# A three-stage decoder: row sums by 32-column matmuls and a VectorE transpose, four expert weight sets loaded a stage earlier

## The chip, the core and the metric

The kernel runs on one core of one Trainium2 chip. The metric is device time in microseconds of one launch; lower is better. Before the change three runs gave a median of 1043.18 us (1040.03 to 1043.35).

## What is computed

A post-layer-norm decoder layer for x of 4 batches, 512 tokens, 512 features, float32, in three sublayers, each followed by a residual add and a layer norm:

```python
x = _layernorm(x + _L0_attn_ref(x, Wq, bq, Wk, bk, Wv, bv))       # 16 heads of 32: window of 256 keys, all keys for 64 chosen queries
x = _layernorm(x + _L0_xattn_ref(ctx_512, ctx_512, mask, pad_mask, x, Wq, bq, Wk, bk))   # softmax(scores * x), 512x512 per batch
x = _layernorm(x + _L0_ffn_ref(x, gate_w, w_gate, w_up, w_down, sw_gate, sw_up, sw_down))  # top 2 of 8 experts of width 352, and a shared one of 704
```

Softmax needs the sum of each row of exponentials. In attention there are 512 rows and 16 heads per batch, and the sums divide the product of probabilities and values.

## The kernel before

The program has four blocks, one after the other, each with its own list of instructions for every engine, ordered by semaphores: `project` (projections of queries, keys, values and context), `attend`, `cross_and_shared` and `experts`.

**attend** (from L615) works through 16 units, each a batch and a group of 4 heads. Keys lie on partitions. In a unit, TensorE (`unit`, L820) has 16 steps. Step s computes one 128x512 block of transposed scores (L830, called st here), which ScalarE turns into exponentials `probs` (L892); beside it stands one 128x512 block of plain scores (L772) of a unit ahead, of which VectorE takes the maxima (L920, `reduce`), five blocks of them (`EARLY`) one unit further ahead. The maxima of all 16 blocks become shift rows (`row_maxima`, L923), which TensorE turns (`turn`, L775) and ScalarE copies into the queries (`take_shift`). The score blocks go round three PSUM banks. `RING` is 17: the seventeenth place of a unit is used for its row sums (`rows_bank`), so each unit's first two scores wait for the score two before them and its third for the reciprocal.

At chosen steps TensorE also does the finishing work of the unit before. `weigh` (L783) is the value product, 4 matmuls with 32 stationary columns each, that go to four column groups of the array. `sums` (L794) adds up the exponentials: GpSimd adds pairs of probability blocks (L719), and 4 matmuls with a stationary block of ones give every row sum 32 times over, laid out as the output is. The trace shows a float32 matmul as two records. ScalarE copies output and sums to SBUF (`take_out` L874, `take_sum` L879). `back` (L805) then brings both back to tokens on partitions: four transposes of the output (L813), and four matmuls with a 0/1 matrix that pick one sum per head (L812). VectorE takes reciprocals and multiplies (`normalise`, L946).

The order, by step: step 3, `weigh(u-1, 3)` and `sums(u-1, 0)`; step 7, `sums(u-1, 1)`; step 11, `back(u-1)` and `weigh(u, 0)`; step 15, `turn(u+1)`, `weigh(u, 1)`, `weigh(u, 2)`.

**cross_and_shared** goes through 16 tiles of 128 tokens. SP's queue per tile: store of x2 (L1204), load of the input of the tile after next (L1196), store of x3 (L1212). GpSimd reads the input in `add_attn` (L1229), then computes masks and the roots of the layer norms in order. After the last tile SP loads the weights of expert 0 (`load_expert`, L1086: four DMAs, together 2.1 MB).

**experts** goes through 39 tiles of 128 gathered rows, sorted by expert. SP first issues ten lists of rows (L1755), waits for the first four gathers, and loads experts 1 to 7, each when the one before has landed (L1763 to L1766). GpSimd issues the gathers (L1791) and the scatter-adds (L1797) and clears the unused rows of the weights (L1808). ScalarE and VectorE split the weights of each tile into two halves (L1825, L1893), ScalarE applies the gate activation (L1833), TensorE does 33 matmuls and 7 transposes a tile.

The attention results, the context parts (`qk_ctx`) and, in the first two blocks, the values `v` share SBUF with `w_all`, the weights of all experts.

## Time and profile before

| what | value |
|---|---|
| median of 3 runs | 1043.18 us (1040.03 to 1043.35) |
| the profiled execution's own time | 1040.61 us |
| its span in the trace | 1038.9 us |
| TensorE busy (PE) | 929.5 us, 89% |
| VectorE busy (DVE) | 750.2 us, 72% |
| ScalarE busy (ACT) | 594.4 us, 57% |
| GpSimd busy (POOL) | 523.3 us, 50% |
| attention stage | about 180 to 449 us |
| cross and shared stage | about 449 to 713 us |
| expert stage | about 713 to 1039 us |
| mean granted TensorE clock | 0.954 |

A share of the whole span says little here, as the stages have different limits; a stage is read from its own stretch. Start and length of an instruction are in microseconds from the start of the span. In the timeline equal neighbours are merged: "x8" is eight records from the first's start to the last's end. Matmuls are pipelined, so the distance of two starts, not a length, is the cost of one.

### The profile page before, as it was taken

How to read it: one execution, taken by the hardware profiler on the slowest of the kernel's cores; microseconds unless marked ns; L12 is line 12 of the kernel's file. 1: busy time of each engine (PE TensorE's matmuls, PEld its weight loads, DVE VectorE, ACT ScalarE, POOL GpSimd, SP SyncE). 2: the span in 40 equal slices, each digit the busy share in tenths (PEclk: the TensorE clock that was granted, in tenths of full speed). 3: DMA queues.
4: the chain of work that ended last, by engine and by line, in shares of the span. 5: the costliest groups of instructions: out<-in, count | busy, mean ns of one | idle time of the engine just before them, and what ended most of it. 6: DMA issues, size and time to landing. Idle time of an engine off the chain costs nothing. (4 is left out here: it accounts for less than half of the span.)

```text
span 1038.9 us, 18144 instructions
## 1 busy us (share of the span) xinstructions
PE 929.5 (89%) x5112; PEld 715.9 (69%) x5112; DVE 750.2 (72%) x1348; ACT 594.4 (57%) x914; POOL 523.3 (50%) x532
## 2 busy tenths in 40 slices
PE   7999997899999999938999999992887999999980
PEld 5777885455554545417988888982876998988970
DVE  4427555777777777459888888744877999999983
ACT  4533211677767777725434434431866888888863
POOL 3550001466666666455555665524143667786634
PEclk9999998899999999968999999996999999999995
DMA  8657301625344256011111111132798444444476
GB/s 280 241 190 224 142 1 38 143 64 121 92 90 120 62 121 186 28 33 64 63 62 62 41 51 61 51 115 49 235 274 231 74 70 79 81 71 73 79 184 212
DMA packets 80885, 115.73 MB, mean 111 GB/s; under 512 B 15681, under 2 KB 37057, under 8 KB 80833
## 3 DMA queue, kind: packets, MB, share of 16 engines
q1 hardware_dynamic: 68960, 93.58, 30.4%
q0 software_dynamic: 9760, 20.49, 10.9%
q10 hardware_dynamic: 2112, 1.05, 0.4%
q8 instruction: 23, 0.38, 0.2%
q14 instruction: 30, 0.24, 0.1%
HBM read 74.77 MB, written 40.31 MB: 111 GB/s over the span
## 5 line engine op out<-in xcount | busy, mean ns | idle before, releaser
L1893 DVE TENSOR_TENSOR we_lo<-w_all,we_hi 128x1408 fp32r<-128x1408 f32 (+1 forms) x117 | 192.6, 1674 | 13.6 <-ACT we_hi L1825 12.9
L920 DVE TENSOR_REDUCE maxima<-ps_s 128x8 f32<-128x512 f32 x240 | 148.9, 684 | 54.7 <-PE ps_s L772 54.5
L1825 ACT ACTIVATE we_hi<-w_all 128x1408 fp32r (+1 forms) x117 | 165.9, 1421 | 37.0 <-PE e_ps_y L1966 20.1
L719 POOL TENSOR_TENSOR pair_sum<-probs 128x512 f32<-128x512 f32 x120 | 150.0, 1279 | 68.9 <-ACT probs L892 68.9
L892 ACT ACTIVATE probs<-ps_st 128x512 f32<-128x512 f32 x256 | 134.3, 602 | 56.5 <-PE ps_st L830 54.9
L1797 POOL DMA_INDIRECT x_dram<-e_y,who x39 | 103.2, 2646 | 124.8 <-ACT e_y L1842 80.0
L1563 PE MATMUL ps_gu<-sw_hi,x2T_hi 128*128 128x352 f32 (+1 forms) x256 | 87.7, 343 | 2.6 <-issue 1.7
L1563 PE MATMUL ps_gu<-sw_lo,x2T_hi 128*128 128x352 f32 (+1 forms) x256 | 83.7, 327 | 0.0
L1563 PE MATMUL ps_gu<-sw_hi,x2T_lo 128*128 128x352 f32 (+1 forms) x256 | 83.4, 326 | 0.0
L772 PE MATMUL ps_s<-k_more,q_more 96*128 96x512 f32 x160 | 67.9, 429 | 4.1 <-DVE maxima L920 2.2
L1791 POOL DMA_INDIRECT xg<-x_dram,who x39 | 61.2, 1568 | 14.3 <-issue 11.1
L830 PE MATMUL ps_st<-q_more,k_more 128*128 128x512 f32 x160 | 67.5, 424 | 0.2 <-ACT probs L892 0.2
L790 PE MATMUL ps_o<-probs,vu 128*32 128x512 f32 x512 | 64.8, 601 | 0.0
L830 PEld LDWEIGHTS ps_st<-q_more,k_more 128*128 128x128 f32 x160 | 30.1, 189 | 40.8 <-issue 23.9
L1966 PE MATMUL e_ps_g<-we_hi,xgT_hi 128*128 128x352 f32 x156 | 55.0, 353 | 3.3 <-DVE we_lo L1893 3.3
L343 DVE SCALAR_TENSOR_TENSOR qk_ctx<-ps_proj,bias_qk,qk_ctx 128x512 fp32r<-128x512 f32 x32 | 24.0, 751 | 46.0 <-ACT attn L276 28.4
L1966 PE MATMUL e_ps_u<-we_hi,xgT_hi 128*128 128x352 f32 x156 | 53.8, 345 | 0.0
L270 ACT ACTIVATE qk_ctx<-ps_proj,bias_qk 128x512 fp32r<-128x512 f32 x32 | 22.1, 689 | 54.8 <-PE ps_proj L457 53.9
L1563 PEld LDWEIGHTS ps_gu<-sw_hi,x2T_hi 128*128 128x128 f32 x256 | 48.7, 190 | 5.5 <-issue 3.5
L1966 PE MATMUL e_ps_g<-we_lo,xgT_hi 128*128 128x352 f32 x156 | 51.9, 332 | 0.0
L1966 PE MATMUL e_ps_g<-we_hi,xgT_lo 128*128 128x352 f32 x156 | 51.7, 332 | 0.0
L1340 ACT ACTIVATE act_g<-ps_gu 128x352 f32<-128x352 f32 x32 | 14.9, 464 | 62.9 <-PE ps_gu L1563 62.6
(272 smaller groups left out, 2484.3 us busy)
## 6 DMA issues: line engine op xcount, KB each, us to landing
qk_dram<-qk_ctx SPq DMA_DIRECT2D x32, 512.0 KB, 3.0
q_more<-qk_dram SPq DMA_DIRECT2D x60, 128.0 KB, 3.0
k_more<-qk_dram SPq DMA_DIRECT2D x60, 128.0 KB, 3.1
w_all<-in_L_ffn_w_gate_dram SPq DMA_DIRECT2D x8, 704.0 KB
w_all<-in_L_ffn_w_up_dram SPq DMA_DIRECT2D x8, 704.0 KB
q_first<-qk_dram SPq DMA_DIRECT2D x36, 128.0 KB, 3.2
k_first<-qk_dram SPq DMA_DIRECT2D x36, 128.0 KB, 3.4
x_tile<-in_x_dram SPq DMA_DIRECT2D x16, 256.0 KB, 2.7
```

What stands on the lines that cost most here:

```text
L719: last = pool.tensor_tensor(pair_sum[:, h, j], probs[:, 2 * h, j], probs[:, 2 * h + 1, j], ALU.add)
L772: pe.matmul(bank(p, x), q4[p][0:BR, j, t * P:(t + 1) * P], k4[p][0:BR, j, :], start=True, stop=True).then_inc(s_done, 1)
L790: last = pe.matmul(ps_o[HD * j:HD * (j + 1), :], vu[:, kc, HD * j:HD * (j + 1)], probs[:, kc, j, :], start=(kc == 0), stop=(kc == TT - 1))
L830: pe.matmul(st_bank(p, s), k4[p][:, j, kc * P:(kc + 1) * P], q4[p][:, j, :], start=True, stop=True).then_inc(st_done, 1)
L892: act.activation(probs[:, kc, j, :], st_bank(p, s), ACT.Exp, scale=SCALE).then_inc(exp_done, 1)
L920: dve.tensor_reduce(by_tile[:, t, j, 1:9], bank(p, x).rearrange("p (g n) -> p g n", n=S // 8), axis=AX.X, op=ALU.max).then_inc(s_reduced, 1)
L1563: last = pe.matmul(out, stationary[a](q), moving[z](q), start=(q == 0 and k == 0), stop=(q == chunks - 1 and k == 2))
L1791: pool.indirect_dma_start(out=xg[:, j % XG, :], out_offset=None, in_=x2_dram[:], in_offset=bass.IndirectOffsetOnAxis(ap=who[:, j, 0:1], ax ...
L1797: pool.indirect_dma_start(out=x3_dram[:], out_offset=bass.IndirectOffsetOnAxis(ap=who[:, j, 0:1], axis=0), in_=y[:, p, :], in_offset=None, ...
L1825: act.activation(w_hi[kind][:], raw(base, kind), ACT.Copy).then_inc(s[kinds[kind] + "_hi"], 1)
L1893: dve.tensor_tensor(w_lo[kind][:], raw(base, kind), w_hi[kind][:].bitcast(F32), ALU.subtract).then_inc(s[kinds[kind] + "_lo"], 1)
L1966: last = pe.matmul(out, stationary[a](q), moving[z](q), start=(q == 0 and k == 0), stop=(q == chunks - 1 and k == 2))
```

## The change

In attention the row sums are computed once per row instead of 32 times: the stationary operand is one column of ones among 32 (`head_col`), one for each head, and each of 4 column groups takes 128 tokens, so the sums of all four heads and all tokens lie in a 128x128 block. VectorE transposes its 32x32 blocks to `sum_rows` and takes the reciprocal; ScalarE's copy and the four matmuls of `back` go. The bank place for the row sums goes too, so scores use all three banks without exception. The second `sums` moves from step 7 to step 11, ahead of `weigh(u, 0)`, and `back` from step 11 to step 15, ahead of `turn`. VectorE's row work is split in two, with the first reduction of the next unit in between, and the normalisation moves behind that unit's first five reductions.

SBUF is laid out anew: `v` first (over the space of the early loads), then the context parts batch by batch, then the attention results; `w_all` begins behind the gather buffers `xg`. Experts 0, 1, 2 and 3 are loaded in the cross stage, ahead of SP's work for tiles 2, 12, 14 and 15; experts 4 to 7 in the expert stage as before. The unused rows are cleared in two halves, the kept experts' at the end of the cross stage, the others' behind the fourth gather.

```diff
+def ctx_at(which, part, b):
+
+    return b * (4 * S) + (2 * which + part) * S
...
-        ones = m.sb("ones_sum", [P, HD])
+        head_col = m.sb("head_col", [P, HPG, HD])
         probs = m.sb("probs", [P, TT, HPG, S])
         pair_sum = m.sb("pair_sum", [P, 2, HPG, S])
         outT = m.sb("outT", [P, S])
-        sumT = m.sb("sumT", [P, S])
-        first_rows = m.sb("first_rows", [P, HPG])
+        sum_rows = m.sb("sum_rows", [P, TT, HD])
...
+        ps_total = ps_sum[:, 0:P]
...
-            return ps_s[:, (RING * p + x) % BANKS, :]
-
-        def rows_bank(p):
-
-            return bank(p, NU)[:, 0:TT * HPG].rearrange("p (t j) -> p t j", j=HPG)
+            return ps_s[:, (NU * p + x) % BANKS, :]
...
-                pool.memset(ones[:], 1.0)
                 pool.memset(turn_in[:], 0.0)
-                pool.memset(first_rows[:], 0.0).then_inc(cleared, 1)
+                pool.memset(head_col[:], 0.0).then_inc(cleared, 1)
                 pool.wait_ge(cleared, 1)
-                pool.affine_select(out=first_rows[:], in_=first_rows[:], compare_op=ALU.not_equal, fill=1.0, base=0,
-                                   pattern=[[-HD, HPG]], channel_multiplier=1).then_inc(cleared, 1)
+                for j in range(HPG):
+                    last = pool.memset(head_col[:, j, j:j + 1], 1.0)
+                last.then_inc(cleared, 1)
...
-                    if x < 2:
-                        need(pe, s_reduced, NU * u + x - 1)
-                    elif x == 2:
-                        need(pe, recip_done, u - 2)
-                    else:
-                        need(pe, s_reduced, NU * u + x - BANKS + 1)
+                    need(pe, s_reduced, NU * u + x - BANKS + 1)
                     pe.matmul(bank(p, x), q4[p][0:BR, j, t * P:(t + 1) * P], k4[p][0:BR, j, :],
...
-                        last = pe.matmul(ps_sum[HD * j:HD * (j + 1), :], ones[:], pair_sum[:, h, j, :],
-                                         start=(h == 0), stop=(h == 1))
+                        rows = pair_sum[:, h, j, :].rearrange("p (t a i) -> p a t i", t=TT, i=HD)
+                        for a in range(P // HD):
+                            last = pe.matmul(ps_total[HD * a:HD * (a + 1), :], head_col[:, j, :], rows[:, a],
+                                             start=(h == 0 and j == 0), stop=(h == 1 and j == HPG - 1))
                     last.then_inc(sums_done, 1)
-                def back(u, after, scores):
+                def back(u):
                     pe.wait_ge(o_taken, u + 1)
                     pe.wait_ge(sum_taken, u + 1)
-                    pe.wait_ge(normed, u + 1)
-                    pe.wait_ge(s_reduced, scores)
                     for t in range(TT):
-                        pe.matmul(rows_bank(after)[:, t, :], sumT[:, t * P:(t + 1) * P], first_rows[:], start=True, stop=True)
                         last = pe.transpose(ps_back[:, t * P:(t + 1) * P], outT[:, t * P:(t + 1) * P], c.ident[:])
                     last.then_inc(backed, 1)
...
                         if s == 3 and not first:
                             weigh(u - 1, 3)
                             sums(u - 1, 0)
-                        if s == 7 and not first:
-                            sums(u - 1, 1)
                         if s == 11:
                             if not first:
-                                back(u - 1, (p + 1) % SLOTS, NU * U if last else NU * (u + 1) + 14)
+                                sums(u - 1, 1)
                             weigh(u, 0)
                         if s == 15:
+                            if not first:
+                                back(u - 1)
                             if not last:
                                 turn(u + 1, p)
                             weigh(u, 1)
...
                         sums(u, 0)
                         weigh(u, 3)
                         sums(u, 1)
-                        back(u, (p + 2) % SLOTS, NU * U)
...
+                        back(u)
...
-                def take_sum(u):
-                    act.wait_ge(sums_done, 2 * u + 2)
-                    act.activation(sumT[:], ps_sum[:], ACT.Copy).then_inc(sum_taken, 1)
...
                 def row_maxima(u):
-                    k = [0]
+                    dve.wait_ge(s_reduced, NU * u + NU)
+                    dve.tensor_reduce(m_win[:].rearrange("p t j -> p t j"), windows, axis=AX.X, op=ALU.max)
+                    dve.tensor_reduce(m_all[:], by_tile, axis=AX.X, op=ALU.max).then_inc(row_step, 1)
+
+                def turn_rows(u):
+
+                    k = [1]
                     def step(ins):
                         k[0] += 1
...
                         dve.wait_ge(row_step, 6 * u + k[0])
                     bar = c.bar[:, :, bass.ds(HPG * u, HPG)]
-                    dve.wait_ge(s_reduced, NU * u + NU)
-                    dve.tensor_reduce(m_win[:].rearrange("p t j -> p t j"), windows, axis=AX.X, op=ALU.max)
-                    step(dve.tensor_reduce(m_all[:], by_tile, axis=AX.X, op=ALU.max))
+                    dve.wait_ge(row_step, 6 * u + 1)
                     step(dve.tensor_tensor(m_bar[:], m_all[:], bar, ALU.add))
                     step(dve.tensor_tensor(m_row[:], m_bar[:], m_win[:], ALU.max))
                     need(dve, turned, u)
...
                     step(dve.tensor_copy(bar_rows, bar))
                     dve.sem_inc(turn_ready, 1)
-                def normalise(u, after):
+                def take_sum(u):
+                    dve.wait_ge(sums_done, 2 * u + 2)
+                    dve.transpose(sum_rows[:].rearrange("p t r -> p (t r)"), ps_total).then_inc(sums_turned, 1)
+                    dve.wait_ge(sums_turned, u + 1)
+                    dve.sem_inc(sum_taken, 1)
+                    dve.reciprocal(rsum[:], sum_rows[:, :, 0:HPG]).then_inc(recip_done, 1)
+
+                def normalise(u):
                     dve.wait_ge(backed, u + 2)
-                    dve.reciprocal(rsum[:], rows_bank(after)).then_inc(recip_done, 1)
                     dve.wait_ge(recip_done, u + 1)
                     dve.tensor_tensor(slot(c.attn, u).rearrange("p (t w) -> p t w", w=HD), ps_back[:].rearrange("p (t w) -> p t w", w=HD),
                                       rsum[:].rearrange("p t (j a) -> p (t j) a", a=1).to_broadcast([P, TT * HPG, HD]),
...
                         for x in range(EARLY, NU):
                             reduce(u + 1, (p + 1) % SLOTS, x)
                         row_maxima(u + 1)
+                        if not (isinstance(u, int) and u > U - 3):
+                            dve.wait_ge(row_step, 6 * (u + 1) + 1)
+                            reduce(u + 2, (p + 2) % SLOTS, 0)
+                        turn_rows(u + 1)
+                        if not first:
+                            take_sum(u - 1)
                     else:
                         last_pairs(0)
-                    if not first:
-                        normalise(u - 1, (p + 1) % SLOTS)
+                        take_sum(u - 1)
                     if last:
+                        normalise(u - 1)
                         last_pairs(1)
                     if not (isinstance(u, int) and u > U - 3):
-                        for x in range(EARLY):
+                        for x in range(1, EARLY):
                             reduce(u + 2, (p + 2) % SLOTS, x)
+                    if not first and not last:
+                        normalise(u - 1)
                     if last:
-                        normalise(u, (p + 2) % SLOTS)
+                        take_sum(u)
+                        normalise(u)
                 dve.sem_inc(s_reduced, NU)
                 dve.wait_ge(cleared, 1)
                 row_maxima(0)
+                turn_rows(0)
...
+def unused_rows(c, first, end):
+
+    return c.w_all[FCR:P, first * WCOLS:end * WCOLS].rearrange("p (e n) -> p e n", n=WCOLS)[:, :, WCOLS - D:WCOLS]
...
+                def expert_in(e):
+                    if e:
+                        sp.wait_ge(c.w_in, 64 * e)
+                    load_expert(sp, c, e, w_gate, w_up, w_down, c.w_in)
+
                 def one(n, b, t):
+                    if isinstance(n, int) and n == 2:
+                        sp.wait_ge(s["sw_split"], 6)
+                        expert_in(0)
+                    if isinstance(n, int) and n == NT - TT:
+                        sp.wait_ge(s["sc_done"], 2 * TT)
+                        sp.wait_ge(s["q_tile_done"], 2 * TT)
+                        expert_in(1)
+                    if isinstance(n, int) and n == NT - 2:
+                        sp.wait_ge(s["sc_done"], NT)
+                        sp.wait_ge(s["q_tile_done"], NT)
+                        expert_in(2)
+                    if isinstance(n, int) and n == NT - 1:
+                        sp.wait_ge(s["x3_st"], 16 * n - 16)
+                        expert_in(3)
...
                 tiles(sp, one)
-                sp.wait_ge(s["sc_done"], NT)
-                sp.wait_ge(s["q_tile_done"], NT)
-                load_expert(sp, c, 0, w_gate, w_up, w_down, c.w_in)
...
                 tiles(pool, one)
+                pool.wait_ge(s["sw_split"], 6)
+                pool.wait_ge(s["sc_done"], NT)
+                pool.wait_ge(s["x3_st"], 16 * (NT - 2))
                 pool.iota(plan_tiles.at_i, pattern=[[P, NT]], base=0, channel_multiplier=0)
                 pool.iota(plan_tiles.tile_i, pattern=[[1, NJ]], base=0, channel_multiplier=0).then_inc(s["plan_built"], 1)
                 send(NT - 1, (NT - 1) % 2)
+                pool.memset(unused_rows(c, 0, KEPT), 0.0)
...
+KEPT = 4
...
-                for e in range(1, E):
-                    list_in(e + LISTS - 1, (e + LISTS - 1) % WHO)
+                for e in range(KEPT, E):
+                    list_in(e + LISTS - KEPT, (e + LISTS - KEPT) % WHO)
                     sp.wait_ge(c.w_in, 64 * e)
                     load_expert(sp, c, e, w_gate, w_up, w_down, c.w_in)
-                first = E + LISTS - 1
+                first = E + LISTS - KEPT
...
-                    if j == 1:
+                    if j == 3:
                         pool.wait_ge(s["padded"], 1)
                         pool.wait_ge(half_done, 1)
-                        pool.memset(w[FCR:P, :].rearrange("p (e n) -> p e n", n=WCOLS)[:, :, WCOLS - D:WCOLS], 0.0).then_inc(s["zeroed"], 1)
+                        pool.memset(unused_rows(c, KEPT, E), 0.0).then_inc(s["zeroed"], 1)
...
+                    if isinstance(j, int) and j == 2:
+                        act.wait_ge(s["zeroed"], 1)
...
-                act.wait_ge(s["zeroed"], 1)
...
-            c.w_all = Memory(nc, later).sb("w_all", [P, E * WCOLS])
+            ml = Memory(nc, later)
+            c.xg = ml.sb("xg", [P, XG, D])
+            c.w_all = ml.sb("w_all", [P, E * WCOLS])
         with ExitStack() as ctx2:
             m2 = Memory(nc, ctx2)
-            c.qk_ctx = [[m2.sb(f"qk_ctx{a}{b}", [P, B * S], F32R) for b in range(2)] for a in range(2)]
-            c.attn = m2.sb("attn", [P, U, S])
             with ExitStack() as early:
                 me = Memory(nc, early)
                 c.x2 = me.sb("x2", [P, 2, D])
                 c.x_tile = me.sb("x_tile", [P, 2, D])
                 c.sw_raw = me.sb("sw_raw", [P, RAW, FC * D])
+            c.v = m2.sb("v", [P, U, TT * P])
+            c.ctx_parts = m2.sb("ctx_parts", [P, B * 4 * S], F32R)
+            c.attn = m2.sb("attn", [P, U, S])
             with ExitStack() as ctx3:
                 m3 = Memory(nc, ctx3)
-                c.v = m3.sb("v", [P, U, TT * P])
```

Left out: the same renaming of `qk_ctx` to `ctx_parts` at its other uses, and of arguments that fell away.

## Rows read from the trace of the kernel before

**Rows 1.** Busy time by stage; columns: stretch, each engine with its instructions, clock, DMA share.

```profile
180.00:449.00 269.00, 257.15 (x1520) 130.40 (x1520) 190.22 (x393) 189.90 (x352) 159.15 (x135) 0.98 0.42 101
...
713.00:803.00 90.00, 69.40 (x379) 63.15 (x380) 63.32 (x60) 58.76 (x68) 32.76 (x22) 0.89 0.77 224
```

**Rows 2.** Timeline of TensorE (PE, weight loads PEld) in one unit: start, length, count.

```profile
232.63 0.40 PE L780 MATMUL ps_st<-ident_bf,turn_in 128*128 128x128 bf16 x4
232.95 1.92 PE L790 MATMUL ps_o<-probs,vu 128*32 128x512 f32 x16
...
238.76 0.50 PE L830 MATMUL ps_st<-q_first,k_first 128*128 128x512 f32 x1
...
240.51 0.40 PE L772 MATMUL ps_s<-k_more,q_more 96*128 96x512 f32 x1
240.84 1.07 PE L801 MATMUL ps_sum<-pair_sum,ones_sum 128*32 128x512 f32 x8
240.84 0.16 PEld L801 LDWEIGHTS ps_sum<-pair_sum,ones_sum 128*32 128x32 f32 x8 [0.38 <-issue]
241.84 0.50 PE L830 MATMUL ps_st<-q_first,k_first 128*128 128x512 f32 x1
242.17 0.39 PE L772 MATMUL ps_s<-k_more,q_more 96*128 96x512 f32 x1
...
243.95 0.50 PE L772 MATMUL ps_s<-k_more,q_more 96*128 96x512 f32 x1 [0.20 <-DVE maxima L920]
244.29 0.28 PE L812 MATMUL ps_s<-first_rows,sumT 128*128 128x4 f32 x2
...
246.52 0.50 PE L830 MATMUL ps_st<-q_first,k_first 128*128 128x512 f32 x1
...
248.89 0.40 PE L780 MATMUL ps_st<-ident_bf,turn_in 128*128 128x128 bf16 x4
```

**Rows 3.** Timeline of VectorE (DVE) in the same unit.

```profile
242.60 1.89 DVE L920 TENSOR_REDUCE maxima<-ps_s 128x8 f32<-128x512 f32 x3 [0.59 <-PE ps_s L772]
...
245.11 0.17 DVE L936 TENSOR_TENSOR m_bar<-m_all,bar_kept 128x16 f32<-128x16 f32 x1
...
246.21 0.26 DVE L948 RECIPROCAL rsum<-ps_s 128x16 f32<-128x16 f32 x1
...
247.21 2.48 DVE L920 TENSOR_REDUCE maxima<-ps_s 128x8 f32<-128x512 f32 x4
```

**Rows 4.** Timeline of TensorE in the expert stage, transposes.

```profile
805.86 0.60 PE L1959 MATMUL e_ps_xT<-ident,xg 128*128 128x128 f32 x4
...
808.35 0.49 PE L1986 MATMUL e_ps_gT<-ident,e_g 128*128 128x128 f32 x3
```

**Rows 5.** Timeline of ScalarE (ACT) behind the last unit.

```profile
445.16 0.60 ACT L881 ACTIVATE sumT<-ps_sum 128x512 f32<-128x512 f32 x1 [0.26 <-PE ps_sum L801]
```

**Rows 6.** Timeline of SP's DMA issues, first and last late expert of seven.

```profile
729.30 0.43 SPq L1090 DMA_DIRECT2D w_all<-in_L_ffn_w_gate_dram  x1
...
788.28 0.37 SPq L1090 DMA_DIRECT2D w_all<-in_L_ffn_w_gate_dram  x1
```

**Rows 7.** Timeline of ScalarE in the expert stage, gate activations.

```profile
749.16 0.47 ACT L1833 ACTIVATE e_act<-e_ps_g 128x352 f32<-128x352 f32 x1 [0.34 <-PE e_ps_g L1966]
...
775.21 0.47 ACT L1833 ACTIVATE e_act<-e_ps_g 128x352 f32<-128x352 f32 x1 [0.43 <-DMA w_all<-in_L_ffn_w_down_dram]
...
808.61 0.47 ACT L1833 ACTIVATE e_act<-e_ps_g 128x352 f32<-128x352 f32 x1 [0.42 <-PE e_ps_g L1966]
...
815.45 0.46 ACT L1833 ACTIVATE e_act<-e_ps_g 128x352 f32<-128x352 f32 x1 [0.40 <-PE e_ps_g L1966]
```

**Rows 8.** Timeline of GpSimd (POOL) at the start of the expert stage.

```profile
719.45 3.51 POOL L1808 MEMSET w_all<- 32x4096 f32 x1
```

**Rows 9.** Timeline of SP's DMA issues in the cross stage, input of tile 4.

```profile
497.09 0.43 SPq L1196 DMA_DIRECT2D x_tile<-in_x_dram  x1
```

**Rows 10.** Timeline of GpSimd, where that input is read.

```profile
503.89 1.28 POOL L1229 TENSOR_TENSOR r<-x_tile,attn 128x512 f32<-128x512 f32 x1
```

22 lines of the change are left out of this document (10 added, 12 removed).

## The prediction

> **What bounds the kernel now.** I read the busy shares by stage first, then one attention unit instruction by instruction on TensorE and on VectorE, then the expert stage tile by tile, and last the queues that feed it. TensorE is busy 257 of the 269 us of attention, but only 69 of the first 90 us of the expert stage, where the DMA engines are at 0.77 [rows 1]. So the one stage is a matter of TensorE's order, the other of transfers.
>
> A unit of attention runs from one group of turned shifts to the next, 232.63 to 248.89, 16.26 us [rows 2]; twelve such units stand in a row. TensorE has hardly a gap in it. Three pieces are touched. The second sums, alone between two score steps, take 240.84 to 241.84. Eight narrow records last 1.07 and sixteen 1.92, so eight stream for 0.86; the other 0.14 is the change in and out. The score at 243.95 is late: VectorE's maxima release it. The back group, row-sum matmuls and transposes in turn, starts at 244.29, and with a value product behind it (0.86 and 0.14) it reaches the next step at 246.52: 1.23 us of its own. VectorE does three reductions in 1.89 us and four in 2.48, so 0.60 apart and 0.69 alone, and between 244.49 and 247.21 has a serial tail of maxima, rows, reciprocal and normalisation [rows 3].
>
> **The attention part.** I follow the unit from its step 4, 238.76.
> - Steps 4 to 11 now run without sums between them. A step costs TensorE 0.47 ((240.51 - 238.76 - 0.33)/3, the first score coming 0.33 after its step) and VectorE 0.60, so the reductions bind. The first score is at 239.09, its reduction 0.43 later as at 242.17 and 242.60 [rows 2, 3]. With the bank slot for the row sums gone every score needs the reduction three before it, the eighth the fifth: 239.52 + 4 x 0.60 + 0.69 = 242.61, so it starts at 242.67. Before it was at 243.95, less 1.00 of sums 242.95. Gain 0.28.
> - The second sums now stand directly ahead of the first value product: 242.67 + 0.33 (as 240.51 to 240.84) = 243.00, then 2 x 0.86 + 0.12: step 12 at 244.84, not 246.52 [rows 2]. In this are the 1.23 of the back group and 0.14 for the change that falls away.
> - VectorE decides what is left. Its last reduction ends at 239.52 + 6 x 0.60 + 0.69 = 243.81. The maxima take 0.62 with their wait (244.49 to 245.11 before). The first reduction of the next unit now slips in, 244.43 to 245.12; the rest of the rows 1.10 (245.11 to 246.21), to 246.15; then the new transpose of the sums and the reciprocal, 0.26 [rows 3]. The transpose is in no row. It moves 128 elements a partition: at least the 0.26 of the reciprocal's 16, at most the 0.69 of a whole bank's reduction. I take 0.31, since its size is nearer the small end, and 0.1 for its own wait. The second reduction ends at 246.15 + 0.41 + 0.26 + 0.69 = 247.51. Step 15's score needs it: 247.55, not 244.84 + 0.33 + 3 x 0.47 = 246.6. So 0.9 us of the gain become a wait for VectorE.
> - Four transposes go ahead of the turn. Four take 0.60 and three 0.49 in the expert stage [rows 4], so each costs 0.11: 0.45 in place of 1.23. Turn at 247.55 + 0.34 + 0.45 = 248.34, not 248.89: **0.55 us a unit**, 8.3 for fifteen.
> - ScalarE loses a copy of 0.60 a unit that nobody waits for inside the loop. At the very end it is on the path: 0.60 and the wait of 0.26 ahead of it [rows 5] and 0.78 of the back group, less 0.5 for the transpose and its wait: 1.1.
> - The sums stream as many columns, but in 16 logical matmuls of 128 a call instead of 4 of 512: 32 records, not 8. If the four column groups still stream side by side that is 0.86 again. I add 0.05 a call; the second call's surplus lies under the wait just named (cover 0.9), the first one's doesn't: 16 x 0.05 = 0.8. The other end: the back group's twelve small records take 1.23, 0.10 each, so 3.3 a call.
> Attention: 8.3 + 1.1 - 0.8 = **8.6 us less**. In the last unit the normalisation of unit 14 waits for transposes four steps later and stands ahead of the last pair sums on VectorE; two value products and the first sums on TensorE cover it. I cost it at nothing; uncovered it is about 0.7 once.
>
> **The weights.** Before, expert 0 is loaded behind the cross stage and experts 1 to 7 from 729.30 on, the last issued at 788.28: 9.8 us apart [rows 6]. An undisturbed tile takes 6.84 (gate activations 808.61 to 815.45 [rows 7]). From 749.16 to 775.21 three tiles take 26.05, 5.5 too many; from 775.21 to 808.61 four take 33.40, 6.0 too many: gathers and scatter-adds queue behind weights. Now experts 1 to 3 come in the cross stage and four remain. POOL's memset of 3.51 us [rows 8] moves behind the first four gathers at half its size, and SP, which waits for these gathers ahead of its loads, starts some 3 us earlier; four loads end near 766. The first loss stays, the second goes: **6.0 us less**. Bounds: 11.5 if both go, 0 if the loss only moves.
> The earlier loads share SP's queue with the cross stage. Ahead of tile 2, four issues of 0.6 and some 9 us of data (an expert's spacing, [rows 6]) now precede an input load that was issued at 497.09 and read at 503.89 [rows 9, 10]. From about 495.5 that makes it land near 507, 3 us late. POOL's chain for the next tiles, VectorE's normalisation and TensorE's transposes follow it. The same comes again ahead of tile 12; tiles 14 and 15 load no input. Price: 0 to 6 us. I take **2 us more**, as each stage of the chain has some room and TensorE is its last. The memset for the kept experts (half of 3.51) lies beside VectorE's table planning.
>
> **Sum.** -8.6 - 6.0 + 2 = -12.6. The profiled execution took 1040.61 us (span 1038.9), so 1028.0. It lies 2.6 below the median of the runs, 1043.18, and 0.6 above the fastest; the next median lies up to 2.6 above its sum. I forecast 1029.
>
> **The rivals.**
> - Short matmuls don't overlap (slower). Place: the 32 records of each sums call. For the cheap price: a call's eight weight loads last 0.16 together [rows 2], so eight are issued at once; no row shows 32. At 0.10 each a call takes 3.3, 2.4 more: 16 first calls pay 39, 16 second ones 1.5 each behind the cover, 24; 1029 + 63 = 1092. It decides from about 1.75 us a call, 55 ns a record: 16 x 0.9 = 14 eat the gain. Chance 0.09 beyond that, 0.03 close to it.
> The Trainium skill, "TensorE: Matmul & The Clock Gate" (Back-to-back issue gap), speaks for this rival: with hardware decode off the sequencer spends about 62 ns on each MATMUL, which binds for short ones. By it a call takes 32 x 0.062 = 1.98 us and the whole 1029 + 18 + 4 = 1051. The eight loads at once are against it, but a queue filled in advance would look the same.
> - VectorE's chain is longer: a transpose of 0.69, or a larger wait for it. Each 0.4 costs 15 x 0.4 = 6: 1035. Chance 0.08.
> - The prefetch only moves the collisions: the experts gain nothing and the cross stage loses 5: 1029 + 6 + 3 = 1038. For it: rows 7 show that a tile suffers wherever weights flow. Against: the intervals are 6.84 as soon as the loads end. Chance 0.10.
> - The loads come no earlier, as SP waits for the shared weights' split or an old store: 1029 + 6 - 2 = 1033. Chance 0.02.
> The forecast itself, 1022 to 1034, has 0.68.
>
> **Numbers.** A measurement of this kernel tells 0.3%, about 3 us, from no change. Faster: 0.68 + 0.08 + 0.10 + 0.02 = 0.88, less 0.04 for causes unseen: 0.84. Same 0.06, slower 0.10. The range goes from 1019 (both expert losses gone and no price in the cross stage) to 1040 (chain or collisions, and the runs' spread); some 0.12 lie above, 0.06 below.
>
> **What would show it.** Right: a unit of 15.6 to 15.8 us; a sums call of 0.9; at step 15 a score released by VectorE's maxima; gate activations 6.84 apart from about 767 of the old clock on; expert loads behind the stores of tiles 1, 11 and 13 in the cross stage; input reads of tiles 4 and 14 released by a DMA. Wrong: sums records more than 0.05 apart; a unit over 16; tiles that lose 1.5 us behind the last late load; two or more long tiles in the cross stage.

## The result and the profile after

Four runs of the changed kernel gave a median of 1031.66 us (1030.36 to 1032.52); four runs of the kernel before beside them, 1042.00. The ratio is 0.9901, 95% interval 0.9879 to 0.9924: about 10 us faster. The forecast was 1029.0, in a range of 1019 to 1040. The profiled execution took 1031.16 us, its span 1029.5. The busy times of each engine over the span follow; the shares say as little as before, only ScalarE has visibly less to do (594.4 us before):

```profile
PE 917.3 (89%) x5752; PEld 726.0 (71%) x5752; DVE 751.7 (73%) x1364; ACT 583.5 (57%) x898; POOL 533.0 (52%) x535
```

A unit of attention in the middle of the loop, as TensorE's timeline of the changed kernel shows it (start, length, engine, line, operation, tile, count, idle before and its releaser), to be held against [rows 2]:

```profile
235.29 0.39 PE L778 MATMUL ps_st<-ident_bf,turn_in 128*128 128x128 bf16 x4
...
240.43 1.06 PE L801 MATMUL ps_sum<-pair_sum,head_col 128*32 128x128 f32 x32
...
248.89 0.40 PE L770 MATMUL ps_s<-k_more,q_more 96*128 96x512 f32 x1
250.19 0.51 PE L770 MATMUL ps_s<-k_more,q_more 96*128 96x512 f32 x1 [0.67 <-DVE maxima L910]
250.53 0.60 PE L810 MATMUL ps_sum<-ident,outT 128*128 128x128 f32 x4
250.97 0.39 PE L778 MATMUL ps_st<-ident_bf,turn_in 128*128 128x128 bf16 x4
```

Turn to turn it takes 15.68 us, where it was 16.26. The 32 small records of a sums call last 1.06, as the eight large ones did (1.07). The score of step 15 is released by VectorE's maxima, and the four transposes take 0.44 to the turn. VectorE in the same stretch, against [rows 3]:

```profile
247.68 0.17 DVE L930 TENSOR_TENSOR m_bar<-m_all,bar_kept 128x16 f32<-128x16 f32 x1
...
248.44 0.20 DVE L937 CAST turn_in<-bar_kept 128x16 bf16 x1
248.87 0.32 DVE L942 STREAM_TRANSPOSE sum_rows<-ps_sum 128x128 f32<-128x128 f32 x1 [0.24 <-DVE turn_in L937]
249.33 0.25 DVE L945 RECIPROCAL rsum<-sum_rows 128x16 f32<-128x16 f32 x1
249.50 2.43 DVE L910 TENSOR_REDUCE maxima<-ps_s 128x8 f32<-128x512 f32 x4
```

The chain is the predicted one: rows, transpose, reciprocal, then the reduction that the score waits for.

The start of attention is not as predicted. The first unit, in the timelines of VectorE, GpSimd and TensorE of the changed kernel:

```profile
199.47 1.16 DVE L934 SCALAR_TENSOR_TENSOR turn_in<-m_row,turn_in 128x16 bf16<-128x16 f32 x1
...
199.25 3.78 POOL L722 TENSOR_TENSOR pair_sum<-probs 128x512 f32<-128x512 f32 x3 [3.65 <-ACT probs L885]
...
201.59 0.50 PE L770 MATMUL ps_s<-k_more,q_more 96*128 96x512 f32 x1 [1.64 <-DVE maxima L910]
202.26 2.90 PE L788 MATMUL ps_o<-probs,vu 128*32 128x512 f32 x16
```

The next turn stands at 201.93. A row step that takes 0.23 elsewhere takes 1.16 beside a pair addition of GpSimd; TensorE stands idle for 1.64; then sixteen records of the value product take 2.90 instead of 1.92. The first unit takes 22.0 us (19.95 before), the second 17.3 (16.25 before). Busy time by stretch shows the clock; the columns are those of [rows 1], and the stretches are the second unit, the unit shown above, and the middle stage:

```profile
201.93:219.24 17.31, 16.61 (x138) 9.45 (x138) 12.02 (x27) 11.26 (x21) 10.11 (x9) 0.90 0.37 83
235.29:250.97 15.68, 15.01 (x138) 8.84 (x136) 12.18 (x27) 11.14 (x21) 10.24 (x10) 1.00 0.35 99
...
461.94:680.63 218.69, 211.59 (x1190) 189.32 (x1191) 175.61 (x456) 94.69 (x170) 125.39 (x200) 0.98 0.27 85
```

In the middle stage the loads of expert 0 and expert 1 delay the input, as GpSimd's timeline says of tile 4 and of tile 14 (against [rows 10]). Between the two stands a second wait, on VectorE in tile 2, for GpSimd's small writes to the table of rows (`table_dram`) to land. The start of each tile on ScalarE, the x2 copies of tiles 2 and 3 and of tiles 12 and 13, shows what they cost:

```profile
499.56 1.29 POOL L1259 TENSOR_TENSOR r<-x_tile,attn 128x512 f32<-128x512 f32 x1 [1.67 <-DMA x_tile<-in_x_dram]
505.05 0.17 DVE L1514 TENSOR_REDUCE slot_u<-placed 128x2 uint32<-128x16 f32 x1 [2.72 <-DMA table_dram<-entry,slot_u]
...
645.62 1.29 POOL L1259 TENSOR_TENSOR r<-x_tile,attn 128x512 f32<-128x512 f32 x1 [4.04 <-DMA x_tile<-in_x_dram]
...
492.37 0.59 ACT L1369 ACTIVATE x2T_hi<-ps_xT 128x512 fp32r<-128x512 f32 x1
507.73 0.59 ACT L1369 ACTIVATE x2T_hi<-ps_xT 128x512 fp32r<-128x512 f32 x1
...
636.43 0.59 ACT L1369 ACTIVATE x2T_hi<-ps_xT 128x512 fp32r<-128x512 f32 x1
653.22 0.59 ACT L1369 ACTIVATE x2T_hi<-ps_xT 128x512 fp32r<-128x512 f32 x1
```

Tile 2 takes 15.36 us (14.27 before), tile 12 takes 16.79 (13.44 before). Tile 3 gives 0.4 back and tile 13 gives 0.7, so the two pairs of tiles cost 0.7 and 2.6. In tile 2 the wait that ends last is the one for the table's writes: the normalisation behind it starts at 505.44, and GpSimd's roots for it were ready at 504.65. The clock is not part of it: in both places it stays at 1.00. From first to last of these copies the stage takes 218.7, before 215.3. In the expert stage the gate activations keep the first loss of [rows 7] and are free of the second:

```profile
745.12 0.47 ACT L1868 ACTIVATE e_act<-e_ps_g 128x352 f32<-128x352 f32 x1 [0.34 <-PE e_ps_g L2002]
756.63 0.47 ACT L1868 ACTIVATE e_act<-e_ps_g 128x352 f32<-128x352 f32 x1 [2.67 <-PE e_ps_g L2002]
765.27 0.47 ACT L1868 ACTIVATE e_act<-e_ps_g 128x352 f32<-128x352 f32 x1 [1.39 <-PE e_ps_g L2002]
772.70 0.47 ACT L1868 ACTIVATE e_act<-e_ps_g 128x352 f32<-128x352 f32 x1 [1.01 <-PE e_ps_g L2002]
```

The 9.4 us between the two spans, by such marks: up to the last turn 3.9 gained, from there to the first x2 copy 2.2 gained, middle stage 3.3 lost, from there to the first gate activation 0.5 lost, gate activations 5.1 gained, the end behind the last of them 2.2 gained (35.2 us after 37.4).

### The profile page after: what moved, and what is told of

It reads as the page before. It is cut to its first block and busy times, and to the rows that moved or that the text cites. A ratio compares the mean times of both kernels' runs of the same rounds, so it can differ in the third digit from the quotient of the medians.

```text
span 1029.5 us, 19458 instructions
## 1 busy us (share of the span) xinstructions
PE 917.3 (89%) x5752; PEld 726.0 (71%) x5752; DVE 751.7 (73%) x1364; ACT 583.5 (57%) x898; POOL 533.0 (52%) x535
## 3 DMA queue, kind: packets, MB, share of 16 engines
q10 hardware_dynamic: 2112, 1.05, 0.4%
## 5 line engine op out<-in xcount | busy, mean ns | idle before, releaser
L1929 DVE TENSOR_TENSOR we_lo<-w_all,we_hi 128x1408 fp32r<-128x1408 f32 (+1 forms) x117 | 192.4, 1673 | 12.6 <-ACT we_hi L1860 11.7
L1832 POOL DMA_INDIRECT x_dram<-e_y,who x39 | 105.8, 2714 | 110.2 <-ACT e_y L1877 80.1
L885 ACT ACTIVATE probs<-ps_st 128x512 f32<-128x512 f32 x256 | 132.2, 604 | 51.4 <-PE ps_st L827 51.0
L1826 POOL DMA_INDIRECT xg<-x_dram,who x39 | 67.6, 1733 | 14.8 <-issue 11.1
L350 DVE SCALAR_TENSOR_TENSOR ctx_parts<-ps_proj,bias_qk,ctx_parts 128x512 fp32r<-128x512 f32 x32 | 24.0, 750 | 46.0 <-ACT attn L283 28.3
L277 ACT ACTIVATE ctx_parts<-ps_proj,bias_qk 128x512 fp32r<-128x512 f32 x32 | 22.1, 690 | 54.7 <-PE ps_proj L464 53.9
L770 PEld LDWEIGHTS ps_s<-k_more,q_more 96*128 96x128 f32 x160 | 31.5, 198 | 30.4 <-DVE maxima L910 23.5
```

Of the source, the lines that this page charges most:

```text
L770: pe.matmul(bank(p, x), q4[p][0:BR, j, t * P:(t + 1) * P], k4[p][0:BR, j, :], start=True, stop=True).then_inc(s_done, 1)
L885: act.activation(probs[:, kc, j, :], st_bank(p, s), ACT.Exp, scale=SCALE).then_inc(exp_done, 1)
L1826: pool.indirect_dma_start(out=xg[:, j % XG, :], out_offset=None, in_=x2_dram[:], in_offset=bass.IndirectOffsetOnAxis(ap=who[:, j, 0:1], ax ...
L1832: pool.indirect_dma_start(out=x3_dram[:], out_offset=bass.IndirectOffsetOnAxis(ap=who[:, j, 0:1], axis=0), in_=y[:, p, :], in_offset=None, ...
L1929: dve.tensor_tensor(w_lo[kind][:], raw(base, kind), w_hi[kind][:].bitcast(F32), ALU.subtract).then_inc(s[kinds[kind] + "_lo"], 1)
```

## The experiments

Below, "unit" is the time from turn to turn inside the loop, "middle stage" the time from the first to the last x2 copy, both from the one profiled execution of each kernel, and the time is the median of all runs with the ratio to the kernel before beside it. The kernel before gave medians of 1041.8 to 1042.6 in these comparisons, single runs 1036 to 1049.

### Each part alone

The first kernel is the one before with the edits to `attend` alone, the second the one before with all the other edits.

> The kernel before with the attention's part of the change alone: the new form and places of the row sums, the transposes at step 15, the new VectorE order, the scores' waits; the buffers' layout and all of the experts' loads stay as before. Theory (the two parts add up, and the attention's share is what the changed kernel shows up to its first x2 norm, which came 6.0 us earlier): about 1036.0, between 1035 and 1037.5, experts' part unchanged from before (gate activations lose 4.7 us at the fifth and 1.7 to 2.7 at three later ones). The two slow first units (22.0 and 17.3 us from turn to turn, where before had 19.95 and 16.25) should be here too if they come from the new order of the steps. Rival (the slow first units come from the moved buffers and the TensorE clock's luck): they are as before here, and the time is 3 us lower, about 1033.

Measured: 1035.03 us (1031.45 to 1036.98), ratio 0.9925 (0.990 to 0.995), inside the theory's range. Units 15.7; first x2 copy at 459.2, before at 468.0, 8.7 earlier. The first unit is slow here too (21.0), the second is not (15.7). The middle stage is as before (215.6).

> The kernel before with the other part alone: buffers laid out anew, the weights of experts 0 to 3 loaded among the tiles of the middle stage, the attention as before. Theory (the parts add up; middle stage +4, experts -5, and the final tail of 2.2 us belongs to the experts' loads): about 1038, between 1036.5 and 1039.5. Rival (the loads only take the places of other traffic, and the final 2.2 us come from elsewhere): 1040 to 1042, no change. Units of attention should take 16.26 us each from turn to turn, as before.

Measured: 1043.87 us (1038.92 to 1047.50), ratio 1.0006 (0.9985 to 1.0027). The rival fits, though the time lies even above its range: alone, the earlier loads bring nothing. In the profiled execution the gate activations take 269.6 us instead of 273.7, 4.1 gained, but the middle stage takes 222.5, 7.2 lost: tiles 2 and 3 take 17.75 and 14.86, tiles 12 and 13 take 17.03 and 13.71. So the attention's edits carry some 8 of the 10 us, and the loads between nothing and 3: the intervals of the ratios allow no closer split.

### What limits a unit now

```diff
                         turn_rows(u + 1)
+                        if not (isinstance(u, int) and u > U - 3):
+                            reduce(u + 2, (p + 2) % SLOTS, 1)
                         if not first:
                             take_sum(u - 1)
...
-                        for x in range(1, EARLY):
+                        for x in range(2, EARLY):
```

> The changed kernel with one more step of VectorE's order moved: the second score reduction of the unit after next goes ahead of the transposing copy and the reciprocal of the row sums, so the score of step 15 no longer waits for them. Theory (the 0.83 us that TensorE waits there each unit lie on the path, and VectorE has the room): the score starts 0.6 to 0.7 us earlier, a unit of 15.7 us becomes 15.0 to 15.2, time 1021 to 1025. Rival (VectorE's chain as a whole bounds a unit, so the wait moves to the next score or to the transposes behind the row sums' copy, now later): units stay at 15.6 to 15.7, time 1030 to 1033.

Measured: 1026.64 us (1022.44 to 1029.61), ratio 0.9841 (0.9814 to 0.9868). Units of 15.17: the wait was on the path and VectorE has the room. From first to last turn it is 10.0 us less than in the changed kernel. The time lies between the two expectations and is not 10 lower, because the middle stage took 224.3 here, with tiles 2 and 3 at 18.6 and 15.0: GpSimd waits 5.5 us for the input there, 1.7 in the changed kernel. Busy time by stretch around that stall shows the clock:

```profile
495.50:499.40 3.90, 0.54 (x5) 0.54 (x6) 1.27 (x3) 0.00 (x0) 2.81 (x5) 1.00 0.00 0
499.40:502.80 3.40, 3.40 (x11) 2.63 (x10) 2.19 (x6) 0.84 (x3) 1.47 (x4) 0.50 0.53 159
```

TensorE worked for 0.54 of 3.9 us and then went on at half clock (1.2 GHz) for 3.4 us. Tiles 2 and 3 take 4.5 us more than in the changed kernel. The wait for the input is 3.8 longer, and 3.4 us at half clock give away 1.7 by an estimate, so the wait is the larger part and the clock the smaller one. Why the input lands so much later here, the runs leave open.

The sums calls doubled:

```diff
-                            last = pe.matmul(ps_total[HD * a:HD * (a + 1), :], head_col[:, j, :], rows[:, a],
-                                             start=(h == 0 and j == 0), stop=(h == 1 and j == HPG - 1))
+                            for twice in range(2):
+                                last = pe.matmul(ps_total[HD * a:HD * (a + 1), :], head_col[:, j, :], rows[:, a],
+                                                 start=(h == 0 and j == 0 and twice == 0),
+                                                 stop=(h == 1 and j == HPG - 1 and twice == 1))
```

> The changed kernel with each of the 32 small matmuls of a row-sum call issued twice into the same accumulation, so the row sums come out doubled; all else as it is. It prices the call. Theory (a call of 32 records takes 0.87 to 0.90 us of TensorE's own time at steps 3 and 11, and both places are on the path that sets a unit): twice 0.8 to 0.9 more a unit, periods of 17.3 to 17.5 us, time 1055 to 1058. Rival 1 (only one of the two places is on the path, the other has cover in VectorE's reductions): periods of 16.5, time 1043 to 1046. Rival 2 (records queue up behind their own weight loads and are dearer when there are more): over 1060.

Measured: 1055.22 us (1051.79 to 1058.17), ratio 1.0117 (1.0087 to 1.0147). TensorE's timeline of one unit:

```profile
239.41 2.00 PE L802 MATMUL ps_sum<-pair_sum,head_col 128*32 128x128 f32 x64
245.66 2.02 PE L802 MATMUL ps_sum<-pair_sum,head_col 128*32 128x128 f32 x64
```

64 records last 2.00 and 32 last 1.06, so 0.94 for 32, 29 ns each. The unit is 16.63, 0.94 longer than 15.69, for two such additions: one call is on the path and the other is covered, as the first rival has it. It is the second that is covered: from turn to second call this unit takes 11.39 (10.46 in the changed kernel), and from there to the next turn 5.23 (5.22). The time of 1055 lies in the theory's range only by chance: from first to last turn it is 11.7 us more than in the changed kernel, under half of what the theory needs. The rest of the 23.6 us does not come from units: the middle stage took 226.3, with stalls of the kind just shown (tile 2: 19.9), and the stretch behind the last gate activation 39.4. With the sums doubled the attention's values are halved, so other rows may go to each expert here, and its expert stage can't be held against the others'.

### Where the second sums stand

```diff
+                        if s == 7 and not first:
+                            sums(u - 1, 1)
                         if s == 11:
-                            if not first:
-                                sums(u - 1, 1)
                             weigh(u, 0)
```

> The changed kernel with the second group of row sums issued at step 7 again instead of step 11; the transposes stay at step 15. Theory (steps 4 to 11 are paced by VectorE's reductions, which TensorE feeds with some 0.1 us to spare a step, so a 0.9 us call among them starves VectorE, while at step 11 it lies beside VectorE's row maxima): a unit 0.3 to 0.6 us longer, time 1036 to 1041. Rival (the pace is VectorE's either way and the banks absorb the call): periods of 15.7, time 1030 to 1033.

Measured: 1090.68 us (1084.92 to 1093.53), ratio 1.0453 (1.0416 to 1.0490). Neither expectation is near. Units take 17 to 22 us. One of VectorE's groups of instructions, from 200 to 400 us of this kernel (busy time, mean ns of one):

```profile
L934 DVE SCALAR_TENSOR_TENSOR turn_in<-m_row,turn_in 128x16 bf16<-128x16 f32 x9 | 10.9, 1210 | 0.3
```

and the same group in the kernel tested next:

```profile
L934 DVE SCALAR_TENSOR_TENSOR turn_in<-m_row,turn_in 128x16 bf16<-128x16 f32 x12 | 2.8, 232 | 0.4
```

One unit of the kernel with the sums at step 7, in the timelines of VectorE, GpSimd and TensorE:

```profile
256.36 1.32 DVE L933 TENSOR_SCALAR turn_in<-m_row 128x16 bf16<-128x16 f32 x1
257.71 1.21 DVE L934 SCALAR_TENSOR_TENSOR turn_in<-m_row,turn_in 128x16 bf16<-128x16 f32 x1
258.80 1.31 DVE L937 CAST turn_in<-bar_kept 128x16 bf16 x1
...
256.35 4.93 POOL L722 TENSOR_TENSOR pair_sum<-probs 128x512 f32<-128x512 f32 x4 [1.06 <-ACT probs L885]
...
261.67 0.80 PE L770 MATMUL ps_s<-k_more,q_more 96*128 96x512 f32 x1 [4.62 <-DVE maxima L910]
```

Four pair additions last 4.93, 1.23 each, and from the moment they run each of the three row steps that are left lasts as long as one of them. TensorE then waits 4.62 us for the reduction behind them, and its score takes 0.80 instead of 0.50: the clock has fallen to half. GpSimd's timeline of the changed kernel shows why it escapes this in its loop:

```profile
242.70 5.01 POOL L722 TENSOR_TENSOR pair_sum<-probs 128x512 f32<-128x512 f32 x4 [1.28 <-ACT probs L885]
248.82 4.98 POOL L722 TENSOR_TENSOR pair_sum<-probs 128x512 f32<-128x512 f32 x4 [1.11 <-ACT probs L885]
```

Its row steps stand from 247.68 to 248.64, in the gap of 1.1 us between the two groups of additions. By the order of the steps, the sums call at step 11 holds back steps 12 to 15, so the exponentials and the second group, but not the reductions and the row steps. At step 7 it is the reductions that it holds back, so that the row steps begin at 255.95, and nothing holds back the second group, which begins at 256.35. The Trainium skill, "SBUF — State Buffer" (SBUF: two separate sides), states the rule: a VectorE operation with two SBUF inputs or in a two-port mode and a GpSimd operation take a shared port pair by an exclusive lock, and the other blocks until it is given back. The trace agrees: 1.16 to 1.32 us for steps of 0.20 to 0.23, while the reductions beside the same additions, which read PSUM, keep their 0.68. The steps of L933 and L937 have one SBUF input, and that they run in a two-port mode no row shows.

To test this, the row steps were put ahead of the reduction in every unit, with the sums at step 7:

```diff
-                        if not (isinstance(u, int) and u > U - 3):
+                        turn_rows(u + 1)
+                        if not (isinstance(u, int) and u > U - 3):
                             dve.wait_ge(row_step, 6 * (u + 1) + 1)
                             reduce(u + 2, (p + 2) % SLOTS, 0)
-                        turn_rows(u + 1)
```

> The kernel with the second row sums at step 7 (which took 1090.7 us) with VectorE's row steps ahead of the reduction of the unit after next in every unit. Theory (those 59 us are row steps that meet the second group of pair additions and last 1.2 us each; a step of 0.7 us earlier they fit ahead of it): row steps back to 0.2 us, periods of 16.0 to 16.6 us instead of 17 to 22, time 1036 to 1046. Rival (the call among steps 4 to 11 is dear by itself): periods of 18 us or more, over 1065.

Measured: 1041.52 us (1036.23 to 1048.03), ratio 1.0012 (0.9986 to 1.0039). Row steps of 0.17 to 0.23 again and units of 16.4: 49 of the 59 us were the meetings with GpSimd and what followed from them, the half clock included. What is left, 0.7 us a unit, lies in this kernel's other order, sums among steps 4 to 11 and the reduction behind the rows; the two were not tested apart.

### The first units

```diff
+                            if first:
+                                weigh(u, 1)
+                                weigh(u, 2)
                             if not last:
                                 turn(u + 1, p)
-                            weigh(u, 1)
-                            weigh(u, 2)
+                            if not first:
+                                weigh(u, 1)
+                                weigh(u, 2)
```

> The changed kernel; in the first unit alone TensorE does the second and third value products ahead of the transposes of the next unit's rows. Theory (the second stretch at half clock, 203.1 to 206.5 us, follows the 1.64 us idle ahead of it, and is what makes the first two units 3.1 us slower than before): idle shorter than 1 us there, no granted clock under 1 after that point, first two periods together 37 us or less, time 1028.5 to 1029.5. Rival (the dip is not of that idle, or VectorE's slow 1.16 us row step sets the pace whatever TensorE does): time within 0.7 us of 1031.7, half-clock stretch still there.

Measured: 1036.70 us (1030.61 to 1045.30), ratio 0.9950 (0.9926 to 0.9974). A miss: the idle time stands ahead of the step's score, which waits for VectorE, and the value products come behind that score, so they filled nothing (the idle stays 1.6 us) and only put off the turn. First unit 24.5 us, a stretch of half clock from 200.8 to 204.2. The profiled execution took 1033.64; what the slower ones did, up to 1045, no trace shows.

```diff
+                        if first:
+                            turn_rows(u + 1)
                         if not (isinstance(u, int) and u > U - 3):
                             dve.wait_ge(row_step, 6 * (u + 1) + 1)
                             reduce(u + 2, (p + 2) % SLOTS, 0)
-                        turn_rows(u + 1)
+                        if not first:
+                            turn_rows(u + 1)
```

> The changed kernel with VectorE's old order in the first unit alone: the five row steps ahead of the reduction of the unit after next. Theory (a short VectorE step that meets one of GpSimd's 1.28 us pair additions lasts until that addition ends; the reduction put ahead pushed the fourth row step of the first unit into the first pair addition, 1161 ns instead of 229): that step back to 0.23 us, TensorE's idle there back from 1.64 to about 0.5 us, first period 19.9 to 20.2 us instead of 22.0, second at 15.7, time 1028.5 to 1030. Rival (the first unit is slow because of its late loads and half clock): first period stays at 21 us or more, time as the changed kernel's, 1031 to 1032.5.

Measured: 1034.23 us (1027.21 to 1039.95), ratio 0.9925 (0.9901 to 0.9950). The row step and the idle time are as expected; the first unit (21.8 us) and the time are not. VectorE's and TensorE's timelines:

```profile
199.21 0.23 DVE L934 SCALAR_TENSOR_TENSOR turn_in<-m_row,turn_in 128x16 bf16<-128x16 f32 x1
...
187.29 1.22 PE L770 MATMUL ps_s<-k_more,q_more 96*128 96x512 f32 x2 [3.28 <-DMA k_more<-qk_dram]
200.48 0.50 PE L770 MATMUL ps_s<-k_more,q_more 96*128 96x512 f32 x1 [0.66 <-DVE maxima L910]
```

The step is 0.23 again, the idle 0.66, the second unit 15.7. But the first unit also holds a wait for a load (3.28 us above), which the rival named: its first score came 7.7 us behind the first turn here, 6.9 in the changed kernel, 6.0 before, and 5.7 to 7.2 in the others. Kernels that don't differ up to that score have waits of 1.3 to 3.3 us there, so I take it for a difference of executions. Counted from that score to the next turn, the first unit takes 13.97 before and in the kernel with the loads alone, 15.06 in the changed kernel and 14.89 with the attention's edits alone, 14.13 here: the meeting costs 0.9 to 1.1 us. The rest of this kernel's excess lies in the middle stage (222.4, with 3.6 us at half clock behind each of the two stalls).

### The collisions of the loads

```diff
                         load_x(n + 2, t)
+                    if isinstance(n, int) and n == 2:
+                        sp.wait_ge(s["sw_split"], 6)
+                        expert_in(0)
+                    if isinstance(n, int) and n == NT - TT:
+                        sp.wait_ge(s["sc_done"], 2 * TT)
+                        sp.wait_ge(s["q_tile_done"], 2 * TT)
+                        expert_in(1)
```

with the same lines taken out ahead of the wait for x2.

> The changed kernel with the loads of experts 0 and 1 put behind the next tile's input load on SP's queue instead of ahead of it. Theory (the middle stage's 3.9 us are GpSimd's waits for that input, 1.7 us at tile 2 and 4.0 us at tile 12, and the half-clock stretches that such a stall can bring): both waits gone, the stretch from first to last x2 transpose back from 218.7 to 215 to 216, time 1027.5 to 1029. Rival (the expert's 2.1 MB collide with whatever is in flight, with the table's small writes next): another wait takes their place, the stretch stays at 217.5 or over, time 1031 or more.

Measured: 1030.25 us (1027.79 to 1033.13), ratio 0.9884 (0.9853 to 0.9915): between the two, and no measurable gain over the changed kernel. Tile 12 is cured (13.92). Tile 2 is not (16.34): GpSimd no longer waits for the input, but VectorE still waits 1.9 us for the table's writes to land, as it did 2.7 in the changed kernel, where that wait and not the input's ended last. Theory right at one tile, rival at the other.

What the clock adds to a stall can be read from tile 12 and tile 13, where eight kernels have the loads ahead of the input and a wait for it of 3.8 to 4.4 us. In two of them, the changed kernel and the one with the loads alone, the clock stays at 1.00, and the two tiles take 30.5 and 30.7 us; in the other six it falls for 3.6 us, and they take 31.6 to 32.0. So the half clock costs about 1.1 us there, of 2.6 to 4.2 that the two tiles lose against the 27.9 before. TensorE's timeline of tile 12 in the changed kernel, without the fall, and in the kernel with the sums at step 7 and the rows first, with it:

```profile
651.53 0.66 PE L1653 MATMUL ps_xT<-ident,x 128*128 128x128 f32 x4 [2.15 <-DVE x L1462]
653.19 0.40 PE L1637 MATMUL ps_y<-sw_hi,gT_lo 128*128 128x512 f32 x1
...
658.05 0.66 PE L1653 MATMUL ps_xT<-ident,x 128*128 128x128 f32 x4 [1.98 <-DVE x L1462]
659.89 0.63 PE L1637 MATMUL ps_y<-sw_hi,gT_lo 128*128 128x512 f32 x1
```

The same instructions stand behind an idle time of 2.15 us at full clock and behind one of 1.98 at half.

Both moves together, with the second reduction even ahead of the row steps in the first unit:

```diff
                             reduce(u + 2, (p + 2) % SLOTS, 0)
+                            if first:
+                                reduce(u + 2, (p + 2) % SLOTS, 1)
                         turn_rows(u + 1)
```

> The changed kernel with the second reduction ahead of the row sums' copy (in the first unit ahead of the row steps too) and the input loads ahead of the loads of experts 0 and 1. Theory (the two gains are of separate stages and add up; the kernel with the reduction moved lost 4 us more in its middle stage than the changed one, which this takes away): attention from first to last turn 231 to 232 us, first unit under 21 us, middle stage 215 to 216, time 1017 to 1020. Rival (earlier stages only shift what collides): 1024 or more.

Measured: 1026.38 us (1023.27 to 1027.71), ratio 0.9850 (0.9822 to 0.9878). The time is the rival's, for another reason. The middle stage is 217.2, some 1 us more than expected (tile 2 takes 16.33 again), units are 15.15, but the first two take 23.7 and 17.8. The first unit's row steps on VectorE, and the pair additions:

```profile
197.88 1.14 DVE L930 TENSOR_TENSOR m_bar<-m_all,bar_kept 128x16 f32<-128x16 f32 x1
199.06 1.18 DVE L931 TENSOR_TENSOR m_row<-m_bar,m_win 128x16 f32<-128x16 f32 x1
200.28 1.21 DVE L933 TENSOR_SCALAR turn_in<-m_row 128x16 bf16<-128x16 f32 x1
201.53 1.21 DVE L934 SCALAR_TENSOR_TENSOR turn_in<-m_row,turn_in 128x16 bf16<-128x16 f32 x1
...
197.71 4.94 POOL L722 TENSOR_TENSOR pair_sum<-probs 128x512 f32<-128x512 f32 x4 [3.65 <-ACT probs L885]
```

Four steps, four additions. These rows and those of the sums at step 7 are where the idea of the meetings came from; the kernels with the row steps early were made after it.

### The best versions

The kernel with three moves has the second reduction ahead of the row sums' copy, the row steps first in the first unit, and the input loads ahead of the experts'. The last one also splits the loads of experts 0 and 1:

```diff
+                    if isinstance(n, int) and n in (2, 3):
+                        sp.wait_ge(s["sw_split"], 6)
+                        load_expert(sp, c, 0, w_gate, w_up, w_down, c.w_in, n - 2)
```

where part 0 is the gate's matrix and part 1 the rest, and likewise for expert 1 at tiles 12 and 13.

> The changed kernel with three moves: second reduction ahead of the row sums' copy, in the first unit the row steps ahead of both, input loads ahead of those of experts 0 and 1. Theory (all three add up): first period 20 us, then 15.2 each, 231 to 232 us from first to last turn, middle stage 217, time 1016 to 1019. Rival (with the row steps of the first unit early something else stalls, or the next units' row steps meet the pair additions): first two periods over 37 us together, time 1023 or more.

> The kernel of the three moves with the loads of experts 0 and 1 each in two parts, the gate's matrix at one tile and the rest at the next. Theory (what is left of the stall at tile 2 is the table's small writes queued among 2.1 MB, 16.3 us instead of 14.3, and half of the bytes leave them time): tiles 2 and 3 within 14.9 us each, middle stage 215 to 216, 1 to 2 us under the kernel beside it. Rival (any part collides as well, now twice): two tiles of over 15 us each, same time or more.

Measured: 1020.14 us (1019.37 to 1021.36), ratio 0.9795 (0.9769 to 0.9821), and 1018.69 us (1016.51 to 1020.70), ratio 0.9778 (0.9750 to 0.9807). The medians lie 1.1 above and inside what was expected. First unit 20.4 and 20.2, of which 14.21 from first score to turn in both, then 15.17 each. The starts of tiles 2 and 3 in the one and in the other:

```profile
481.27 0.59 ACT L1374 ACTIVATE x2T_hi<-ps_xT 128x512 fp32r<-128x512 f32 x1
497.96 0.59 ACT L1374 ACTIVATE x2T_hi<-ps_xT 128x512 fp32r<-128x512 f32 x1
```

```profile
481.34 0.59 ACT L1379 ACTIVATE x2T_hi<-ps_xT 128x512 fp32r<-128x512 f32 x1
495.82 0.59 ACT L1379 ACTIVATE x2T_hi<-ps_xT 128x512 fp32r<-128x512 f32 x1
```

16.69 becomes 14.48, and tile 3, at which the larger part is loaded, takes 14.14: part 0 is 0.7 MB and part 1 is 1.4 MB, a third and two thirds and not the halves of the expectation. VectorE's wait for the table's writes, 2.3 us in the one, is gone in the other, and the middle stage is 215.8, as if nothing was loaded in it. Whether the size of the first part or its place matters was not tested apart. The two ratios' intervals overlap, so the 1.45 us between the medians rest on these rows more than on the times. Against the kernel before the last version is 2.2% faster (1.9 to 2.5), and its median lies 13 us under the changed kernel's.

## Why the prediction was right or wrong

**The unit of attention: right, step by step.** Predicted 0.55 us a unit, measured 16.26 to a mean of 15.72, 0.54. The wait at step 15 was put at 0.9 and is 0.8 (the score starts at 250.19; without the wait it would follow the one before by 0.47, at 249.36). The transpose was taken at 0.31 from between 0.26 and 0.69: it is 0.32. One sum has a slip: 244.43 + 0.69 + 1.10 is 246.22 and not 246.15, which would make the unit's gain 0.48. It came out right as the row steps follow the start of that reduction by 0.60 and not by 0.69 (247.08 and 247.68 in the trace after). Four transposes at 0.45: 0.44. That the wait is VectorE's chain and nothing else, the moved reduction shows: 15.17.

**The short matmuls: the forecast held and the rival fell.** The surplus of a call was put at 0.05. By the lengths it is nothing (1.06 after, 1.07 before), by the doubled calls 0.08 (0.94 for 32 more records, where eight large ones stream for 0.86 [rows 2]); the term fits both. The rival's price was 0.10 us a record, 3.3 a call; the doubled calls show 29 ns a record. The Trainium skill, "TensorE: Matmul & The Clock Gate" (Back-to-back issue gap), has about 62 ns for each with hardware decode off, and otherwise a floor of about 25 ns for those of up to 64 columns. The 29 ns of this trace, for records of 128 columns, rule out the first. The cover of the second call was also right: of two doubled calls the first costs 0.93 and the second nothing.

**The first two units: the step that failed.** "0.55 us a unit, 8.3 for fifteen" took all units for the one that was read. Only 3.6 came, as the first unit took 2.1 more and the second 1.05 more, and the third gained only 0.2. Of the 2.1, 1.1 is the meeting of a row step with a pair addition (15.06 against 13.97), shown by its undoing (14.13), and 1.0 the later load, which seems to vary by execution. The second unit's loss is a stretch at half clock (0.90 over the unit), behind the 1.64 us idle. Four other kernels with the same idle did not fall (attention's edits alone: 21.0 and 15.7), so that it comes at all hangs on more than the idle; what, these runs leave open. The prediction looked at the order of VectorE's steps for what they wait for, and not for what runs beside them on GpSimd.

**The tail: under-sized.** 1.1 predicted, 2.2 measured from the last turn to the first x2 copy, in the changed kernel and in the one with the attention's edits alone. From the start of the last sums to the start of the last normalisation it is 1.2 (3.52 to 2.31), the step that the 1.1 was for. The other 1.0 lies between the last turn and those sums (17.83 to 16.85): the sixteenth unit gains as well, and the sum counted fifteen.

**The expert stage: right, slightly over-sized.** 6.0 predicted, 5.1 measured (4.1 with the loads alone): the first loss stays at 11.5, the second is gone, but the tiles behind the first loss still take 8.6 and 7.4.

**The middle stage: right place, wrong size.** "I take 2 us more": 3.3 measured, 7.2 with the loads alone, inside and beyond the bounds of 0 to 6. The term "3 us late" was mis-sized in two ways. At tile 12 GpSimd waits 4.0 for the input and the two tiles there lose 2.6, so the room in the chain takes up no more than 1.4. At tile 2 it waits 1.7, and what the 0.7 there hangs on in the end is the table's writes, for which VectorE waits 2.7 us and which the prediction did not have. Other kernels lose more with the loads in the same place: tiles 2 and 3 together took 28.6 to 29.2 us in four kernels whose clock stayed up, the changed one among them, and 31.8 to 35.2 in four whose clock fell; but three of these four also waited 4.7 to 6.8 us for the input, and the clock by itself is worth about 1.1, as tile 12 shows. In the loads alone 7.2 is lost and 4.1 gained, which as a balance is nearer to the rival "the prefetch only moves the collisions" (price in the middle 5, chance 0.10) than to the forecast, though the experts do gain, which the rival denies.

**The sum.** -12.6 predicted and -9.4 in the spans: attention and its tail brought 6.0 instead of 8.6, loads and experts 1.2 instead of 4.0 (0.5 of the loss at the border of the stages), and 2.2 came at the very end of the kernel, where nothing was predicted. That stretch took 35.2 to 37.4 us in all kernels but the doubled one, the kernels without any change to it included, so I read no effect into it. The forecast lay 2.7 below the median; without those 2.2, which are luck of the profiled execution, the sum of the spans would have been 5.4 short and not 3.2.

## What to carry to other kernels

A moved instruction is not only ordered by its semaphores: on VectorE look at what GpSimd runs at that moment, since a 0.2 us step can take 1.2, and the room for it can be as small as the 1.1 us between two groups of additions. A unit read from the middle of a loop says nothing of the first. A large load beside small urgent transfers should be cut so that its parts fit between them: 2.1 MB at once cost two tiles 0.2 to 6.8 us, the same in two parts, in the one kernel that had them, nothing that shows.
